# One AdaLN block on one core: where the second half's right passes, the second modulation and two transposes stand in the order

## What is computed

```python
mod = (_silu(L0_c) @ L0_wmod).reshape(B, 6, 1, -1)
sa, ca, ga, sb, cb, gb = (mod[:, k] for k in range(6))
h = _layernorm(x) * (1 + ca) + sa
# _L0_attn_ref(h):
xn = rmsnorm(h, norm1_w)
left = gelu(xn @ left_W + left_b)
v = causal_depthwise_conv(xn @ right_W + right_b, conv_w, conv_b)
r = sigmoid(v @ ga_W + ga_b); i = sigmoid(v @ gx_W + gx_b)
log_a = -8 * softplus(a_param) * r
a = exp(log_a); mult = sqrt(-expm1(2 * log_a))
hh = associative_scan(a, mult * i * v)          # h[t] = a[t] h[t-1] + b[t]
x1 = (left * hh) @ out_W + out_b + h
x1n = rmsnorm(x1, norm2_w)
y = (gelu(x1n @ up1_W + up1_b) * (x1n @ up2_W + up2_b)) @ down_W + down_b + x1
x = x + bounded(ga) * y
h = _layernorm(x) * (1 + cb) + sb
x = x + bounded(gb) * moe(h)                    # top 2 of 8 experts, plus h
```

## Time and profile before

| | |
|---|---|
| three timed runs, us | 304.69, 307.43, 307.59 |
| the profiled execution, us | 304.61 |
| its span from first to last instruction, us | 302.9 |
| mean granted TensorE clock | 0.976 |
| busy: PE / weight loads / DVE / ACT / POOL, us | 274.6 / 231.5 / 194.0 / 186.3 / 113.0 |

### The profile page before, as it was taken

How to read it: one execution, slowest core, us unless ns; L and a number is a source line. 1 busy time by engine, 2 the same in 40 slices (tenths; PEclk the granted TensorE clock), 3 DMA queues, 4 the chain that set the end, 5 groups by cost and what they waited for, 6 DMA issues and landing times.

```text
span 302.9 us, 4493 instructions
## 1 busy us (share of the span) xinstructions
PE 274.6 (91%) x1607; PEld 231.5 (76%) x1607; DVE 194.0 (64%) x450; ACT 186.3 (61%) x303; POOL 113.0 (37%) x97
## 2 busy tenths in 40 slices
PE   0799999899999999997798979999999999999980
PEld 0695546378588888785476979999999999999980
DVE  4866737929927365978392676768686867686520
ACT  5166679784296335755851869494949494959200
POOL 6000000000124123507475400838475656657562
PEclk9999999999999999999759999999999999999997
DMA  7970000000004766432135943675758392918133
GB/s 240 381 221 0 2 1 0 0 2 0 0 2 153 233 170 123 86 126 92 54 98 170 285 169 112 210 198 179 232 156 255 126 286 87 280 10 209 26 40 38
DMA packets 32727, 38.26 MB, mean 126 GB/s; under 512 B 7989, under 2 KB 28333, under 8 KB 32685
## 3 DMA queue, kind: packets, MB, share of 16 engines
q1 hardware_dynamic: 26816, 29.90, 31.7%
q0 software_dynamic: 4928, 7.44, 11.0%
q10 hardware_dynamic: 956, 0.59, 0.7%
HBM read 31.96 MB, written 8.90 MB: 135 GB/s over the span
## 4 chain that ended last, share of the span: by engine, by line
PE 41%; ACT 4%; issue 2%; DVE 1%; DMA 1%; POOL 1%; POOLq 1%; another core or an unknown queue 0%; ACTq 0%; DVEq 0%
PE bank L892 17%; PE bank L913 14%; PE bank L657 3%; PE bank L878 2%; PE bank L908 2%; PE bank L907 2%; PE bank L802 1%; DMA out_x<-y_tok,meta 1%; ACT own L1208 1%; POOL out_x L1828 1%; POOLq L188 1%; ACT hT L1086 1%; ACT own_raw L1202 1%; DVE xe_lo L1669 0%; ACT L1105 0%
## 5 line engine op out<-in xcount | busy, mean ns | idle before, releaser
L1828 POOL DMA_INDIRECT out_x<-y_tok,meta x24 | 51.0, 2127 | 50.5 <-DVE y_tok L1691 43.9
L913 PE MATMUL bank<-w_hi,own 128*128 128x256 f32 x256 | 47.9, 285 | 0.0
L892 PE MATMUL bank<-xe_hi,w_hi 128*128 128x320 f32 x128 | 39.7, 310 | 3.3 <-DVE xe_lo L1669 3.3
L1673 DVE TENSOR_TENSOR own<-own_raw,own 128x256 fp32r<-128x256 f32 x64 | 27.2, 425 | 23.3 <-ACT own L1208 17.9
L913 PEld LDWEIGHTS bank<-w_hi,own 128*128 128x128 f32 x256 | 40.4, 191 | 0.4
L1202 ACT ACTIVATE own_raw<-bank,b1c 128x320 f32<-128x320 f32 x64 | 33.9, 529 | 9.7 <-PE bank L892 9.7
L892 PE MATMUL bank<-xe_lo,w_hi 128*128 128x320 f32 x128 | 39.6, 309 | 0.0
L892 PE MATMUL bank<-xe_hi,w_lo 128*128 128x320 f32 x128 | 39.6, 309 | 0.0
L913 PE MATMUL bank<-w_lo,own 128*128 128x256 f32 x128 | 36.2, 283 | 0.0
L1208 ACT ACTIVATE own<-own_raw 128x320 fp32r<-128x320 f32 x64 | 28.7, 460 | 0.0
L1818 POOL DMA_INDIRECT gb_rows<-gb_table,meta x24 | 23.4, 974 | 11.6 <-issue 6.7
(11 more groups left out here) (226 smaller groups left out, 626.9 us busy)
## 6 DMA issues: line engine op xcount, KB each, us to landing
e_raw<-in_L_ffn_w SPq DMA_DIRECT2D x16, 1024.0 KB
x_rows<-in_L_attn_x SPq DMA_DIRECT2D x1, 2560.0 KB
xe_tok<-x_rows SPq DMA_DIRECT2D x8, 256.0 KB
raw_m<-in_L_attn_up_W SPq DMA_DIRECT2D x2, 768.0 KB, 9.9
x_tok<-in_L_attn_x SPq DMA_DIRECT2D x2, 512.0 KB, 5.0
out_x<-x_tok SPq DMA_DIRECT2D x1, 1024.0 KB
wmod<-in_L_wmod SPq DMA_DIRECT2D x1, 768.0 KB, 12.2
raw_m<-in_L_attn_down_W SPq DMA_DIRECT2D x1, 768.0 KB, 13.1
```

Source lines behind the costliest of these rows:

```text
L892: ins = nc.tensor.matmul(bank[b][:, 0:CAP], l, r, start=(c == 0 and t == 0), stop=(c == KD - 1 and t == 2))
L913: ins = nc.tensor.matmul(bank[b][0:n, 0:D], l, r, start=(c == 0 and t == 0), stop=(c == KE - 1 and t == 2))
L1673: nc.vector.tensor_tensor(own_lo[e % 2][:, f, :], own_raw[:, f % 4, 0:whole], own_hi[e % 2][:, f, 0:whole].bitcast(F32), ALU.subtract)
L1828: nc.gpsimd.indirect_dma_start(out_rows, bass.IndirectOffsetOnAxis(ap=ids[0:n, e, k, E:E + 1], axis=0), y_tok[e % 2][0:n, k, :], None, com ...
```

## The change

On ACT, `right(1, 0)` goes ahead of the decays of half 0 and `right(1, 1)` between the two blocks of them. On PE, `mod_b`, `gb` and `b1` leave their place between `side("left", 1, 1)` and `gates(1)`: `mod_b` goes behind `out_products(0)` where the six fillers `busy 6` stood, `gb` and `b1` go behind `mean_square2(0)` where the two fillers `busy 4` stood, and both groups of fillers are dropped. DVE's copies of the three, with the scaling of `gate_w`, follow to the matching places. `wmod` is split in two tiles, of which only the first shares memory with `y_all`. The banks behind shift by two; the explicit bank numbers of a later stage are written relative to it, so that the banks' order among themselves stays.

```diff
@@ order of the banks @@
-    for key in ["mod_b", "gb", "b1"]:
-        order.take(key)
     take_gates(1)
     take_out(0)
-    order.take(("busy", 6), drains=0)
+    order.take("mod_b")
     order.take(("ms2", 0))
-    order.take(("busy", 4), drains=0)
+    order.take("gb")
+    order.take("b1")
     order.take(("rb2", 0), drains=2)
@@ memory @@
-        wmod = at("wmod", o_r1 + 4 * TB, [KD, GB * D])
+        wmod_a = at("wmod_a", o_r1 + 4 * TB, [KD, 2 * D])
+        wmod_b = at("wmod_b", o_r1 + 5 * TB, [KD, (GB - GA) * D])
@@ PE @@
             side("left", 1, 1)
+            gates(1)
+            pe.wait_ge(a_in[4], 16)
+            out_products(0)
+            wm_ready(2)
+            any_w = wm_hi[:, 0]
             pe.wait_ge(wmod2_in, 16)
-            modulation("mod_b", range(2 * GA, 2 * GB))
+            modulation("mod_b", wmod_b, 2 * GA, range(2 * GA, 2 * GB))
+            mean_square2(0)
             pe.wait_ge(wmod3_in, 16)
             b, ps = begin("gb")
...
             transposes("b1", lambda j: rows_e[0:E * KE, :], 1, E * KE)
-            gates(1)
-            pe.wait_ge(a_in[4], 16)
-            out_products(0)
-            wm_ready(2)
-            any_w = wm_hi[:, 0]
-            stay_busy(("busy", 6), any_w, 6)
-            mean_square2(0)
-            stay_busy(("busy", 4), any_w, 2)
             spread2(0)
             stay_busy(("busy", 5), any_w, 12)
@@ ACT @@
             act.wait_ge(softplus_done, 1)
-            decays(0)
             right(1, 0)
+            decays(0, [0])
             right(1, 1)
+            decays(0, [1])
             roots(0)
@@ DVE @@
             conv(2)
             conv(3)
+            st.need(ready)
+            recur(0)
+            recur(1)
+
+            st.need(inputs(1))
+            x1_of(0)
             b, ps = full("mod_b")
...
+            rms_inverse(("ms2", 0), 0, 3)
             b, ps = full("gb")
...
             b, ps = full("b1")
...
-            st.need(ready)
-            recur(0)
-            recur(1)
-
-            st.need(inputs(1))
-            x1_of(0)
-            rms_inverse(("ms2", 0), 0, 3)
             rms_apply(("rb2", 0), 0, ("out", 1), "norm2_w")
```

More of the change, by code:

```diff
@@ L169, in adaln_block @@
     order.take(("cwT", 0))
-    order.take(("busy", 1), drains=0, bank=6)
-    order.take(("xh2", 1, 0), drains=2, bank=6)
+    after_weights = order.next
+    order.take(("busy", 1), drains=0, bank=after_weights)
+    order.take(("xh2", 1, 0), drains=2, bank=after_weights)
     order.take(("xh2", 1, 1), drains=2)
     order.take(("places", 1))
-    order.take(("busy", 3), drains=0, bank=4)
-    order.next = 1
+    order.take(("busy", 3), drains=0, bank=(after_weights + 6) % 8)
+    order.next = (after_weights + 3) % 8
     order.take(("h2t", 1, 0))
-    order.take(("h2t", 1, 1), bank=4)
+    order.take(("h2t", 1, 1), bank=(after_weights + 6) % 8)
     take_biases(0)
@@ L449, in _ @@
             load_m(1)
-            sp.dma_start(wmod[:, :, 2 * D:], packed(I["L0_wmod"])[:, :, 2 * D:GB * D]).then_inc(wmod2_in, 16)
+            sp.dma_start(wmod_b[:], packed(I["L0_wmod"])[:, :, 2 * D:GB * D]).then_inc(wmod2_in, 16)
             sp.dma_start(wmod_gb[:], packed(I["L0_wmod"])[:, :, GB * D:]).then_inc(wmod3_in, 16)
@@ L600, in _, with modulation @@
             until_drained("cT")
-            def modulation(key, js):
+            def modulation(key, w, first, js):
                 b, ps = begin(key)
@@ L606, in modulation @@
                     for k in range(KD):
-                        ins = nc.tensor.matmul(ps[:, j * B:(j + 1) * B], wmod[:, k, j * P:(j + 1) * P], cT[:, k, :],
+                        ins = nc.tensor.matmul(ps[:, j * B:(j + 1) * B], w[:, k, (j - first) * P:(j - first + 1) * P], cT[:, k, :],
                                                start=(k == 0), stop=(k == KD - 1))
@@ L610, in _ @@
             pe.wait_ge(wmod_in, 16)
-            modulation("mod_a", range(2 * KD))
+            modulation("mod_a", wmod_a, 0, range(2 * KD))
             def x_blocks(key, hf, src):
@@ L947, in _ @@
             act.dma_start(c_row[0:B, :], I["L0_c"]).then_inc(c_in, 16)
-            act.dma_start(wmod[:, :, 0:2 * D], packed(I["L0_wmod"])[:, :, 0:2 * D]).then_inc(wmod_in, 16)
+            act.dma_start(wmod_a[:], packed(I["L0_wmod"])[:, :, 0:2 * D]).then_inc(wmod_in, 16)
             act.dma_start(a_col[:].rearrange("p (k o) -> p k o", o=1), I["L0_attn_a_param"].rearrange("(k p o) -> p k o", p=P, o=1),
@@ L1012, in gate_functions, with decays @@
                     nc.scalar.activation(tmp[:, 4 * g + hf * KH + m, :], ps[:], ACT.Sigmoid, bias=C(bias, m)).then_inc(drained[b], 1)
-            def decays(hf):
-                for k in range(hf * KH, (hf + 1) * KH):
-                    m = k % KH
+            def decays(hf, ms=range(KH)):
+                for m in ms:
+                    k = hf * KH + m
                     until_drained(("gate", hf, m, 0))
```

## The result

The changed kernel took 308.62 us in the median of 22 runs (305.00 to 310.56), the kernel before, run beside it 22 times, 306.13 us (304.37 to 307.59). Ratio 1.0054, 95% interval 1.0028 to 1.0081; the ratio leaves the most disturbed executions of either kernel out, so it is smaller than that of the medians. In a second comparison on one chip, further down, the ratio was 1.0100 (1.0065 to 1.0135). The change made the kernel slower, by 0.5 to 1%. The profiled execution took 308.81 us.

A forecast was written before the change was run, and what follows sets the result against it. PE's own queue was taken to bound the stretch up to the first up product. From 304.61 us, -0.1 for gain against added queue and +3.7 for a clock fall gave 308.2 us; range of all runs 304.2 to 311.0.

The forecast's parts named there:

- The forecast mechanism: Norm chain: only small products from 61.2 to 65.6 us, so PE's granted clock falls near 65.6; chance 0.55.
- the sign of being wrong as a whole: Behind 80 us, where the order is unchanged: a changed time there would refute the prediction as a whole.
- The gain: Ahead of the out products: gates(1) 1.3 us earlier, recurrence and out products 1.45 us earlier.
- the two parts: Right passes earlier on ACT: 1.3 us for gates(1); mod_b, gb, b1 out of the way: recurrence 1.45 us earlier in all.
- the sum: PE's row times from out products to first up product: 13.3 us instead of 11.85, so 1.45 us added.
- The term -0.1: First up product: 1.45 us won against 1.45 us added on PE's queue, taken as -0.1 us, bounds -1.45 and +0.5.
- The price of the fall: Norm chain at half rate: gb and b1 +1.2, spread +0.92, fillers +1.65; +3.7 us in all, bounds 1.7 and 5.1.
- The base: Whole kernel: the profiled execution's 304.61 us, taken as the starting level instead of the median 307.43.
- rival 1: Norm chain: no clock fall, PE's queue takes back what was won; 304.5 us, chance 0.22.
- rival 2: PE's new pause, 47.55 to 50.35: clock falls there and stays low, slowing gates(1); 310.6 us or more, chance 0.15.
- Rival 3: Norm chain: small products cost no more than the eight fillers did, so 1.45 us stay won; 303.1 us, chance 0.08.

The follow-up runs named there:

- chain dense: Changed kernel with mod_b in PE's pause ahead of gates(1), twelve fillers in its place behind the out products, twelve behind the spread; 307.27 us, ratio 1.0031.
- ACT part alone: Kernel before with only ACT's new order of right passes and decays; 307.62 us, ratio 1.0040.
- all small ahead: ACT's new order; mod_b, gb, b1 ahead of gates(1) as before, eight fillers back, ten behind the spread, DVE's copies moved; 307.99 us, ratio 1.0027.
- second profile: Changed kernel run again unchanged, in a later set of 12 runs on one chip; 309.46 us, ratio 1.0100 to the kernel before.
- PE part alone: Changed kernel with ACT's order as before, so only the PE and DVE moves remain; 310.74 us, ratio 1.0115.
- eight fillers less: Kernel before with only the norm chain's eight fillers removed (six behind the out products, two ahead of the spread); 308.86 us, ratio 1.0065.

## Why the prediction was right, and where its steps were not

**The forecast mechanism is one of those that were found.** A fall near 65.6 was forecast; it came at 66.3, 64.0, 64.4, 63.4 and 65.9 in the five profiles that have `mod_b` whole in the chain. Two pairs bear on what it is due to: dense work in `mod_b`'s place (chain dense) takes 1.6 us out of the chain and 1.35 off the median, and dense work taken from the old chain adds 1.3 us there and 2.6 to the median. The five sets with `mod_b` whole in the chain have medians of 308.6 to 310.9 us and 24.5 to 26.6 us at the low clock; the five that take it or half of it out of the changed kernel's chain have 306.0 to 308.0 and 19.2 to 24.0. But small products without a filler are not a condition: the clock also fell between 64 and 68 us in five of the eight profiles without `mod_b` whole in the chain, two of them with fillers on either side of the sums (ACT part alone, all small ahead). So they seem to make the fall likelier (five of five profiles against five of eight); that they alone bring it is not shown.

**Part of the time changed where the prediction said that it must not.** A change of the time behind 80 us, where the order is the same, was named as the sign of being wrong as a whole. Of the 4.2 us between the two profiled executions 2.0 lie there, with the fall at 179. The forecast had no term for it. The changed stretch itself accounts for 2.2 us in one profile and, counted from the first gates, 4.5 in the other.

**The gain was right within 0.3 us.** Gates 1.16 us earlier (1.3 forecast), out products 1.16 (1.45). ACT's roots started at 50.73, not 50.6, and `recur(0)` at 51.47, not 51.2. What the split of the two parts got wrong stands with the ACT part alone: it holds 0.9 of the 1.16 us.

**PE's queue was 0.35 us longer than the sum.** 1.45 us were added by row starts; chain dense shows 1.8. From out start to `mod_b` start PE takes 3.51 us where the fillers followed after 3.11. The rows of before would have given most of it: with `mod_b` behind them, eight dense products take 47.55 - 40.69 = 6.86 us, so four take 3.43. The term -0.1 was thus +0.6: 1.8 added, 1.16 won.

**The price of the fall was mis-sized.** +3.7 was forecast from the assumption that the clock comes back only 3.3 us after dense fillers begin. It came back at 69.8, within the spread, before any filler: `gb` +0.84, the spread +0.60, the sums +0.15, together 1.6 us. The lower bound of that term, 1.7, was nearer. In the second profile, with 6.8 us at the low clock, out to up took 16.75 instead of 13.64: 3.1 us; in PE part alone, with 10.2 us, it took 18.34: 4.7 us. So the term differs from one execution to the next, 1.6 and 3.1 in the two profiles of the changed kernel, and is not one number.

**The base was mis-sized the other way.** I started from the profiled execution, 304.61, and took the median's distance from it for something the clock did elsewhere. 86 runs of the kernel before have medians of 306.2 to 306.8, with 20 us at the low clock against 14.5 in the profiled execution (clock 0.976). +3.6 us was forecast over the base, +2.5 measured. 308.2 is within 0.4 us of 308.62 because a base 1.5 us too low and an effect 1.1 us too high nearly cancel; that closeness is luck.

**The rivals.** No fall (rival 1): none of the 34 executions of the changed kernel has as little time at the low clock as the best of before. Its 304.5 us also left out the 0.7 us by which queue and gain were mis-sized. The pause (rival 2): the clock did fall just behind it, in one of the two profiles, for 3.4 us at a price of 0.76, where 0.8 was worked out; a hold of 9 us or more there was not seen. The Trainium skill (TensorE: Matmul & The Clock Gate, section HAM oscillation) has pauses between bursts of products pull the clock down. The second profile agrees with that, with a pause of 2.76 us and a fall 1.1 us behind it, though the pauses in that section's example are longer; the first profile, with the same pause, has no fall there. Small products in place of the pause had the fall as well, at 50.2, 49.6, 50.0 and 50.6, so idleness is not the condition; with fillers there, alone or mixed with `mod_b`, it did not come, in one profile each. Rival 3: small products weigh what their rows say. Filling the pause did not pay.

**What stays open.** Why 12 fillers in the pause left the median no lower, in six runs; and what decides in one execution whether and where the clock falls: with `mod_b`, `gb` and `b1` ahead of the gates it stayed up there in the profiles of the kernel before, of ACT part alone and of the kernel with eight fillers less, and fell in that of all small ahead. Each kernel but the changed one has one profile only. The share of the fall near 180 us in the medians was not measured, so how much of the +2.5 us is the changed stretch's own is open.

## What to carry to other kernels

Small matrix products keep PE busy in a trace, and its clock can still fall among them: PE went through the changed chain without a gap while it fell. In a chain of waits that is bridged with 1 and 4 column products, filler that nobody reads can be worth 2.6 us in the median, though here it did not keep the clock up in every execution. Before work is moved into the place of fillers, sum what PE's queue then holds: here 2.5 us of filler made room for 3.9 us of products, and the 1.2 us won ahead were gone before the clock had its say. Test each part of a change alone: here the reorder on ACT held 0.9 us of the gain and the reorder on PE all of the added queue. Compare time at the low clock over many executions, not one profile, and look at the stretches that the change does not touch: one low stretch there was worth about as much as the whole change.

## What was not expected of the hardware

The clock fell even with eight fillers in place (ACT part alone, at 65.6). The low stretches seen between 45 and 75 us lasted 3.4, 6.8 or 10.2 us. Those ahead of 55 us mostly began not in the pause or among the small products but 0.3 to 1.2 us into the dense gates behind them. The same program had 18 to 32 us at the low clock from one execution to the next: 308.48 us at a mean clock of 0.964 and 312.53 at 0.949 for the changed kernel. Over its 22 runs a microsecond at the low clock goes with 0.4 us of time, over the 86 of the kernel before with 0.25.
